# The last expert stage written out over its 32 units, with the next batch routed between them

## The reference, cut to what matters

```
scores = sigmoid(xf @ gate_w.T);  biased = scores + expert_bias
_, sel = top_k(biased, 2);        top_scores = take_along_axis(scores, sel)
routed_in = xf[token_ids] * scores_sorted[:, None]
h = square(relu(grouped_mm(bf16(routed_in), bf16(w_up))))
routed_out = grouped_mm(bf16(h), bf16(w_down))
shared_out = square(relu(xf @ shared_w_up.T)) @ shared_w_down.T
x = layernorm(x + routed_out summed over a token's two experts + shared_out)
```

## Time and profile before

| | us |
|---|---|
| median of 3 runs | 2268.89 (2267.15 to 2275.46) |
| the profiled execution | 2276.37 |
| its span | 2274.5 |
| PE busy in the span | 1954.7 (86%) |
| DVE busy | 1663.7 (73%) |
| ACT busy | 1097.9 (48%) |
| POOL busy | 545.5 (24%) |
| last stage, from its first load to the end of the span | 2098.8 to 2274.5 |

### The profile page before, as it was taken

How to read it: one execution, slowest core, us unless ns; L and a number is a source line. 1 busy time by engine, 2 the same in 40 slices (tenths; PEclk the granted TensorE clock), 3 DMA queues, 4 the chain that set the end, 5 groups by cost and what they waited for, 6 DMA issues and landing times. The chain is left out here.

```text
span 2274.5 us, 31782 instructions
## 1 busy us (share of the span) xinstructions
PE 1954.7 (86%) x10146; PEld 1263.0 (56%) x10146; DVE 1663.7 (73%) x4032; ACT 1097.9 (48%) x2397; POOL 545.5 (24%) x624
## 2 busy tenths in 40 slices
PE   8999799956589999489999999998679988893997
PEld 5666644424367777357666766666453444443544
DVE  4555458866628888668899899888444989996576
ACT  3433345533245555166566666555204756663343
POOL 2222124432201222200000000000001777775111
PEclk9999989976689999689999999999858999996888
DMA  2000000020120000000000000000310222222100
GB/s 84 28 28 18 12 29 21 15 101 28 47 95 10 10 20 10 10 19 1 6 15 6 1 15 6 1 6 6 138 63 9 54 56 70 60 62 73 38 28 28
DMA packets 37238, 75.30 MB, mean 33 GB/s; under 512 B 8822, under 2 KB 20286, under 8 KB 36342
## 3 DMA queue, kind: packets, MB, share of 16 engines
q1 hardware_dynamic: 28918, 56.89, 7.2%
q0 software_dynamic: 8192, 16.79, 2.8%
HBM read 58.98 MB, written 14.68 MB: 32 GB/s over the span
## 5 line engine op out<-in xcount | busy, mean ns | idle before, releaser
L1965 ACT ACTIVATE pk_sums<-pk_sum 128x512 f32<-128x512 f32 x448 | 243.3, 596 | 227.1 <-PE pk_sum L2191 214.6
L2067 DVE SCALAR_TENSOR_TENSOR pk_level<-pk_sums,pk_least 128x1024 f32<-128x1024 f32 x256 | 324.0, 1276 | 22.5 <-ACT pk_sums L1965 21.3
L2198 PE MATMUL pk_weights<-product_keys_early_ident,pk_level 128*128 128x128 f32 x2048 | 267.4, 273 | 35.8 <-DVE pk_level L2067 35.8
L2419 POOL DMA_INDIRECT tk_values<-top_keys_values,tk_index x256 | 243.7, 952 | 202.3 <-DVE tk_index L2584 124.8
L2198 PEld LDWEIGHTS pk_weights<-product_keys_early_ident,pk_level 128*128 128x128 f32 x2048 | 232.0, 141 | 102.0 <-issue 66.5
L2735 PE MATMUL tk_to_act<-tk_keys,tk_xT 128*128 128x512 f32 x512 | 236.7, 610 | 30.1 <-ACT tk_scores L2484 29.4
L2735 PEld LDWEIGHTS tk_to_act<-tk_keys,tk_xT 128*128 128x128 f32 x512 | 95.8, 195 | 153.0 <-issue 93.8
L2190 PE MATMUL pk_sum<-pk_lay_rows,pk_partsT 96*128 96x512 bf16 x448 | 170.2, 380 | 0.2 <-ACT pk_sums L1965 0.2
L2191 PE MATMUL pk_sum<-pk_lay_columns,pk_partsT 96*128 96x512 bf16 x448 | 169.2, 378 | 0.0
L1647 PEld LDWEIGHTS er_outs<-experts_early_w,er_hT 128*128 128x128 f32 x1024 | 134.0, 192 | 59.8 <-issue 56.4
L2582 DVE MAX8 tk_best<-tk_scores 128x8 f32<-128x4096 f32 x32 | 141.3, 4416 | 14.9 <-ACT tk_scores L2484 14.9
(11 more groups left out here) (398 smaller groups left out, 3714.4 us busy)
## 6 DMA issues: line engine op xcount, KB each, us to landing
tk_scores<-top_keys_compress SPq DMA_DIRECT2D x1, 4096.0 KB, 15.1
tk_values<-top_keys_values,tk_index POOLq DMA_INDIRECT x256, 2.5
att_x_proj<-x_first SPq DMA_DIRECT2D x4, 512.0 KB, 5.0
att_x_res<-x_first SPq DMA_DIRECT2D x4, 512.0 KB, 4.1
x_after_attention<-att_y SPq DMA_DIRECT2D x4, 512.0 KB, 4.7
moe_x<-x_after_attention SPq DMA_DIRECT2D x4, 512.0 KB, 3.9
x_after_experts<-moe_y SPq DMA_DIRECT2D x8, 256.0 KB, 2.0
lin_x<-x_after_experts SPq DMA_DIRECT2D x4, 512.0 KB, 4.3
```

The costliest lines, as they stand in the source:

```text
L1965: act.activation(sums[:, n % SUMS, half * HALF:(half + 1) * HALF], bank[:], ACT.Copy).then_inc(S.free.sem, 1)
L2067: dve.scalar_tensor_tensor(level[:, n % LEVELS, :], sums[:, n % SUMS, :], least[:, t % 2, h:h + 1], sums[:, n % SUMS, :], ALU.is_ge, ALU.m ...
L2198: ins = pe.matmul(weights[:, ch * P:(ch + 1) * P], level[:, n % LEVELS, ch * P:(ch + 1) * P], ident[:], is_transpose=True, start=h == 0 an ...
L2419: pool.indirect_dma_start(out=values[:, slot, k, :], out_offset=None, in_=c["values"], in_offset=bass.IndirectOffsetOnAxis(ap=index[slot][ ...
```

## The change

The stage does the same work on the same tiles, in another order and with other banks. The loop over batches is gone: every engine's list is written out over `ALL = 32` units, and the steps of the next batch (transposes and copy of x, gates, exponents, scores, shared up products, relu and squares, transposes of the parts) are placed behind given units of the current one. x has three slots, and the residual reads them, so x is loaded once; `xT` and `partsT` have two slots. The down products and the shared down products keep the expert's matrix as weights and move 512 hidden columns; the sum is then transposed (features on partitions), so ACT copies it (`outT`), PE turns it back by 4 float32 transposes into a bank of its own (`turned`), and DVE adds the residual from there. That bank is taken from ring A, which has 2 banks instead of 3. A batch is stored in halves. In the diff, "..." marks what is left out.

```diff
-        to_act = [m.psum(f"to_act{i}", [P, HALF]) for i in range(3)]
+        to_act = [m.psum(f"to_act{i}", [P, HALF]) for i in range(2)]
...
+        turned = m.psum("turned", [P, HALF])
...
         def _(sp):
-            sp.dma_start(x[:], x_in[0]).then_inc(x_loaded.sem, x_loaded.unit)
...
+            def load(b):
+                after(sp, turned_free, (b - 2) * HALVES)
+                sp.dma_start(x[:, b % 3], x_in[b]).then_inc(x_loaded[b % 3], 16)
+
+            def store(b, g):
+                sp.wait_ge(y_ready, b * HALVES + g + 1)
+                sp.dma_start(x_out[b][:, half_of(g), :], y[:, g]).then_inc(stored[g], 16)
+
+            for b in range(3):
+                load(b)
+            for b in range(B):
+                for g in range(HALVES):
+                    store(b, g)
+                if b + 3 < B:
+                    load(b + 3)
...
         def _(pool):
...
+            for n in range(SHARED):
+                square_shared(0, n)
+            for b in range(B):
+                if b > 0:
+                    root(b - 1, 1)
+                if b + 1 < B:
+                    for n in range(SHARED):
+                        square_shared(b + 1, n)
+                root(b, 0)
+            root(B - 1, 1)
...
         def _(act):
...
+            for unit in range(ALL):
+                b, u = divmod(unit, UNITS)
+                more = b + 1 < B
+                for k in range(PER_UNIT):
+                    take_up(unit, k)
+                if more and u in (0, 1):
+                    take_xT(b + 1, u)
+                if u == 1 and b > 0:
+                    take_out(b - 1, 1)
+                if more and u == 2:
+                    exponents(b + 1)
+                if more and u in (4, 5):
+                    for i in range(2):
+                        take_shared(b + 1, 2 * (u - 4) + i)
+                if u == 5:
+                    take_out(b, 0)
+                if more and u == 5:
+                    take_partsT(b + 1)
+            take_out(B - 1, 1)
...
         def _(dve):
...
+            for unit in range(ALL):
+                b, u = divmod(unit, UNITS)
+                more = b + 1 < B
+                if unit + 1 < ALL:
+                    scale(unit + 1)
+                for k in range(PER_UNIT):
+                    square(unit, k)
+                if u == 2 and b > 0:
+                    finish(b - 1, 1)
+                if u == 3 and b > 0:
+                    normalise(b - 1, 1)
+                if more and u == 3:
+                    score_of(b + 1)
+                if more and u == 4:
+                    parts_of(b + 1)
+                if u == 6:
+                    finish(b, 0)
+                if u == 7:
+                    normalise(b, 0)
...
         def _(pe):
...
+            def shared_project(b, g):
+                after(pe, outT_ready, (b - 1) * HALVES + g + 1)
+                for tail in range(2):
+                    units, w = (TAIL, shared_down_tail) if tail else (P, shared_down)
+                    pe.wait_ge(s_hidden_ready, b * SHARED + g * 2 + tail + 1)
+                    pe.matmul(outs[g][:], w[0:units, :], s_hidden[0:units, g * 2 + tail, :], start=tail == 0, stop=False)
...
+            def project_up(unit):
+                pair = unit % PAIRS
+                for k in range(PER_UNIT):
+                    bank = claim_A()
+                    if k < 2:
+                        pe.wait_ge(W.free.sem, W.free.value(0, 2 * unit + k + 1))
+                        pe.matmul(bank[:], up[:, 2 * pair + k, :], scaled[:, (2 * unit + k) % 4, :],
+                                  start=True, stop=True).then_inc(A.full.sem, 1)
+                    else:
+                        for e in range(2):
+                            ins = pe.matmul(bank[0:2 * TAIL, :], up_tail[:, 2 * pair + e, :],
+                                            scaled[:, (2 * unit + e) % 4, :], start=e == 0, stop=e == 1)
+                        ins.then_inc(A.full.sem, 1)
+
+            def project_down(unit):
...
+                    pe.wait_ge(hidden_ready, n + 1)
+                    ins = pe.matmul(outs[g][:], w, hidden[0:units, n % HIDDEN_SLOTS, :], start=False,
+                                    stop=pair == PAIRS - 1 and k == PER_UNIT - 1)
...
+            def turn_out(b, g):
+                half = b * HALVES + g
+                pe.wait_ge(outT_ready, half + 1)
+                after(pe, turned_free, half)
+                for i in range(PER_HALF):
+                    ins = pe.transpose(turned[:, i * P:(i + 1) * P], outT[:, g, i * P:(i + 1) * P], ident[:])
+                ins.then_inc(turned_full, 1)
+
+            for g in range(HALVES):
+                transpose_x(0, g)
+            gates(0)
+            for n in range(SHARED):
+                shared_hidden(0, n)
+            transpose_parts(0)
+            widen(0)
+            shared_project(0, 0)
+            for unit in range(ALL):
+                b, u = divmod(unit, UNITS)
+                more = b + 1 < B
+                if unit + 1 < ALL:
+                    widen(unit + 1)
+                project_up(unit)
+                if unit >= DOWN_LAG:
+                    project_down(unit - DOWN_LAG)
+                if more and u in (0, 1):
+                    transpose_x(b + 1, u)
+                if u == 2 and b > 0:
+                    turn_out(b - 1, 1)
+                if more and u == 2:
+                    gates(b + 1)
+                if u == 3:
+                    shared_project(b, 1)
+                if more and u in (4, 5):
+                    for i in range(2):
+                        shared_hidden(b + 1, 2 * (u - 4) + i)
+                if more and u == 5:
+                    transpose_parts(b + 1)
+                if u == 6:
+                    turn_out(b, 0)
+                if more and u == 7:
+                    shared_project(b + 1, 0)
+            for unit in range(ALL - DOWN_LAG, ALL):
+                project_down(unit)
+            turn_out(B - 1, 1)
```

More of the change, by code:

```diff
@@ L2757, in routed_experts_stage @@
     UNITS = HALVES * PAIRS
+    ALL = B * UNITS
     DOWN_LAG = 2
@@ new lines, in take_shared, with take_partsT @@
+            def take_shared(b, n):
+                units = P if n % 2 == 0 else TAIL
+                act.wait_ge(A.full.sem, A.to_take(0))
+                bank = A.take()
+                after(act, s_hidden_ready, (b - 1) * SHARED + n + 1 if b else 0)
+                act.activation(s_relu[0:units, n, :], bank[0:units, :], ACT.Relu).then_inc(A.free.sem, 1)
+            def take_partsT(b):
+                act.wait_ge(partsT_full, b + 1)
+                act.activation(partsT[:, b % 2, :], parts_bank, ACT.Copy).then_inc(partsT_ready, 1)
@@ new lines, in take_up, with take_out @@
+            def take_up(unit, k):
+                n = unit * PER_UNIT + k
+                units = 2 * TAIL if k == PER_UNIT - 1 else P
+                act.wait_ge(A.full.sem, A.to_take(0))
+                bank = A.take()
+                after(act, hidden_ready, n - 2 * PER_UNIT + 1)
+                act.activation(relu[0:units, n % (2 * PER_UNIT), :], bank[0:units, :], ACT.Relu).then_inc(A.free.sem, 1)
+            def take_out(b, g):
+                half = b * HALVES + g
+                act.wait_ge(out_full, half + 1)
+                after(act, turned_full, half - 1)
+                act.activation(outT[:, g, :], outs[g][:], ACT.Copy).then_inc(outT_ready, 1)
@@ L2894, in _ @@
                 steps.link(dve.tensor_tensor(score[:], score[:], biased[:], ALU.mult))
-                split_in_three(steps, dve, score[:], lambda i: parts[:, :, i * E:(i + 1) * E], rest[:]).then_inc(parts_ready.sem, parts_ready.unit)
-                def scale(u):
-                    g = u // PAIRS
-                    for k in range(2):
-                        dve.wait_ge(W.full.sem, W.to_take(b))
-                        bank = W.take()
-                        dve.tensor_tensor(scaled[:, (2 * u + k) % 4, :], bank[:], xT[:, g * HALF:(g + 1) * HALF],
-                                                    ALU.mult).then_inc(W.free.sem, 1)
@@ L2942, in _, with scale @@
-                finish(1)
-                normalise(1).then_inc(y_ready.sem, y_ready.unit)
-                steps.restart()
+                after(dve, partsT_ready, b)
+                split_in_three(steps, dve, score[:], lambda i: parts[:, :, i * E:(i + 1) * E], rest[:]).then_inc(parts_ready, 1)
+            def scale(unit):
+                b, u = divmod(unit, UNITS)
+                if unit >= 2:
+                    dve.wait_ge(A.full.sem, made_for_A("up", unit - 2, PER_UNIT - 1))
+                dve.wait_ge(A.free.sem, taken_from_A("xT", b, u // PAIRS))
+                for k in range(2):
+                    dve.wait_ge(W.full.sem, W.to_take(0))
+                    bank = W.take()
+                    dve.tensor_tensor(scaled[:, (2 * unit + k) % 4, :], bank[:], xT[:, b % 2, columns_of(u // PAIRS)],
```

(31 more changed lines are left out.)

288 lines of the change are left out of this document (103 added, 185 removed).

## The result

| kernel | median of its runs, us | ratio of after to before, 95% interval |
|---|---|---|
| before | 2268.0 (2261.8 to 2275.5, 6 runs) | |
| after | 2258.2 (2253.8 to 2259.6, 6 runs) | 0.9951 [0.9929, 0.9973] |

The change made the kernel about 10 us faster; 2270 us was forecast. The profiled execution took 2258.22 us (span 2256.4) against 2276.37 (2274.5). Of the 18 us between the two, 2.46 came about ahead of the last stage, whose first DVE cast is at 2096.37 us instead of 2098.83, and 15.7 in it: 160.0 us from that cast to the end instead of 175.7.

The account below looks back on a forecast made before the run. At full clock PE and DVE were both taken to be at their bound before, PE after. The new order's -14, clock falls' +12 and +3 for POOL and stalls made +1 us, applied to the median: 2270 us, range 2253 to 2287.

Parts of the forecast that it names:

- falls behind the gates: Last stage, next batches' gates: 2.6 falls to half clock, 4.7 us each in the mean, 12 us in all.
- The bank: Ring A with 2 banks: the tail product waits for ScalarE, up to tail 1.12 us for 0.45, +0.67 a unit.
- The down products: Each unit's three products of 512 columns instead of 12 of 128: saving 0.02 us a unit, to 0.75.
- rival 4: Down products: weight loads are what the twelve cost, so -0.58 us a unit, -18, 2252 us; chance 0.04.
- The start: Start of the last stage: widening, two shared down products and widening again put the first up product at 2119.2 us.
- The bound: Last stage: PE carries 35.5 us a batch and bounds it; DVE's 28 a batch fits in that.
- rival 3: Last stage: DVE becomes the bound through POOL's squares, all 12 exposed, 1.02 us each: 2280 us; chance 0.11.
- The list: PE's work from the first up product to the last, units plus next batches' extras, at full clock: 128.4 us.
- POOL beside DVE: POOL's 12 squares beside DVE's work: between 0 and 12 us on DVE, 2 us taken on the path.
- its -14: The new order at full clock, from start to finish of the last stage: 2260.5 us, 14.0 less than 2274.5.
- Rival 1: Last stage: the clock holds or falls once, -14 + 2 us at most, 2256 us; chance 0.25.
- Rival 2: Last stage: after a fall the clock stays low through unit 7, 16 us instead of 4.7, 2281 us; chance 0.17.

Follow-up runs that it names:

- old down products and 3 banks: Changed kernel with 12 down products of 128 columns as before, no turning back, third bank in ring A: 2349.5 us, 0.9871 of the kernel before.
- old down products: Changed kernel with 12 down products of 128 columns as before, no turning back, still 2 banks: 2364.7 us (0.9944), again 2367.2 us (0.9949 of the kernel before).
- gates twice: Changed kernel with the 8 gate products of the next batch run twice in a row: 2378.5 us, 0.9998 of the kernel before.
- filling around the gates: Kernel before with 16 extra bf16 products of 512 columns a batch, before, between and after the gates: 2273.9 us, 1.0029 of the kernel before.
- third run of after: The changed kernel itself, unaltered, measured in a third set on another chip: 2372.0 us, 0.9975 of the kernel before.

## Why the prediction was wrong, point by point

The forecast was +1 us, the medians differ by -10. The step that failed is one term of the sum, the clock's: falls behind the gates were to cost 12 us, 4.7 each, and cost 2.9 in the profile, 1.26 and 1.63. A few small terms leaned the same way.

**Right.** *The bank.* +0.62 a unit came for +0.65 (2.82 and 2.85); up to tail 1.08 for 1.12, since ScalarE starts 0.43 us behind the up product and not 0.51. In the loop with 2 banks and the same down products as before a unit takes 2.93, written out 2.85, so writing out gives 0.08 us a unit back; this the prediction had not seen. *The down products*: 0.74 for 0.75. *The weight loads* (rival 4) cost nothing: 12 products in 0.77 us against 3 in 0.74. The Trainium skill, "TensorE: Matmul & The Clock Gate", Back-to-back issue gap, would by its figures for 128 and 512 columns have had the twelve cost more than twice the three, an estimate, and rival 4's 0.58 us a unit came from there alone; here the measurement decides. *The start*: the record of the first up product is missing, but it follows the widening at 2116.12 by 0.53, at 2116.65; with 2.46 us for the earlier stages 2119.1, predicted 2119.2. *The bound*: PE; rival 3 is out.

**The list.** From the first up product to the last, 2116.65 to 2243.93, it is 127.3 us. Less the 2.9 of the two falls (below) that is 124.4, where 128.4 stood: the pairs of float32 products take 1.91 and 1.86 us in chain for 2.0, the gates 1.7 to 1.85 for 1.95, the unit 0.03 less. In one unit of three batches ScalarE's copy of `partsT` comes between, and the tail waits 0.92 instead of 0.47; that is the stall for which 1 us was added, and it is within the 124.4. The end, from the last up product:

```profile
2243.93 0.59 PE L3097 MATMUL moe_to_act<-moe_scaled,moe_up 128*128 128x512 bf16 x2
...
2248.27 0.66 PE L3121 MATMUL moe_turned<-experts_early_ident,moe_outT 128*128 128x128 f32 x4 [0.69 <-ACT moe_outT L2926]
...
2248.96 0.69 DVE L3001 TENSOR_TENSOR moe_r<-moe_turned,moe_x 128x512 f32<-128x512 f32 x1 [0.17 <-PE moe_turned L3121]
```

is 12.5 us to 2256.4, for 4.8 + 8.0.

**POOL beside DVE**, 2 us for nothing. The contention is there, as the earlier trace rows had it, but on a small instruction; DVE and POOL in order of time:

```profile
2136.10 0.23 DVE L236 TENSOR_TENSOR moe_rest<-moe_score,moe_parts 128x64 f32<-128x64 f32 x1
...
2136.59 1.11 DVE L238 TENSOR_TENSOR moe_parts<-moe_rest,moe_parts 128x64 bf16<-128x64 f32 x1
2136.59 2.03 POOL L2870 TENSOR_TENSOR moe_s_hidden<-moe_s_relu 128x512 f32<-128x512 f32 x2 [23.01 <-ACT moe_s_relu L2908]
2137.63 1.27 DVE L2986 TENSOR_TENSOR moe_scaled<-moe_scores_wide,moe_xT 128x512 bf16<-128x512 f32 x2
```

The line L238 takes 0.23 us alone and 1.0 to 1.1 in the three batches where a square stands beside it: 2.6 us more in all. Otherwise the squares fell beside `scaled`, which takes 0.68 us each with them and without; no `hidden` of this profile stood beside one (0.41 to 0.43 us each, all 93 records). And DVE then waits for PE's `scores_wide` all the same, as the list of waits above shows. With old down products and 3 banks the squares do meet `hidden`, some of which take 1.1 to 1.3 us there.

**The clock, the step that failed.** 2.6 falls at 4.7 us were to cost 12 (the mean of the 2.9 and 5.9 that it gave would have been 4.4, 11 in all). The number of falls was nearly right: in the six profiles of kernels that keep the tail's wait on PE (after three times, old down products twice, gates twice) 13 of 18 gate stretches were followed by a fall, 2.2 a run (one of the 18 stood in the long stretch at half clock already); in the four profiles of the written-out order without that wait it was 2 of 12. The price was not. The first fall's unit, in order of time:

```profile
2124.34 1.85 PE L3055 MATMUL moe_gate_bank<-experts_early_gate,moe_xT 128*128 128x8 f32 x16
2126.12 0.60 PE L3088 MATMUL moe_scores_wide<-moe_partsT,moe_lay 24*128 24x512 bf16 x2
2126.66 0.89 PE L3097 MATMUL moe_to_act<-moe_scaled,moe_up 128*128 128x512 bf16 x2
2127.81 1.09 PE L3101 MATMUL moe_to_act<-moe_scaled,moe_up_tail 128*96 128x512 bf16 x2 [0.26 <-ACT moe_relu L2920]
...
2129.97 1.17 PE L3072 MATMUL moe_outs<-moe_s_hidden,xperts_early_shared_down 128*128 128x512 f32 x2
2131.07 1.12 PE L3072 MATMUL moe_outs<-moe_s_hidden,s_early_shared_down_tail 48*128 48x512 f32 x2
2132.12 0.60 PE L3088 MATMUL moe_scores_wide<-moe_partsT,moe_lay 24*128 24x512 bf16 x2
```

From `scores_wide` to `scores_wide` it is 6.00 us; the same unit of batch 3 at full clock takes 4.74 (2216.73 to 2221.47). So this fall costs 1.26 us. It begins at about 2126.8, behind the gates as predicted, and is over at 2130.2, when the float32 pair that was to lift it has run for 0.2 us, not when the pair or the next one has ended. In 3.4 us at half clock no more than 1.7 can be lost, and part of that is hidden here: the tail's wait is 0.26 us instead of 0.47, as ScalarE is no slower. The second fall, from 2164.4 to 2167.8, begins behind the tail, whose wait is 0.47 as ever, and costs more:

```profile
2162.07 0.60 PE L3088 MATMUL moe_scores_wide<-moe_partsT,moe_lay 24*128 24x512 bf16 x2
...
2165.18 1.91 PE L3072 MATMUL moe_outs<-moe_s_hidden,xperts_early_shared_down 128*128 128x512 f32 x2
...
2168.44 0.60 PE L3088 MATMUL moe_scores_wide<-moe_partsT,moe_lay 24*128 24x512 bf16 x2
```

Its unit takes 6.37 us, 1.63 above 4.74. The two falls cost 2.9 us, 9.1 less than the sum had. Of the 13, eleven lasted 3.0 to 3.5 us, one 7, one 14.

The other side of the account held. Of the 51 us at half clock in the stage before, 38 lay in three stretches of 7, 20.5 and 10 us that followed PE's wait for the first `scaled` of a batch (from 2122.7, 2197.7 and 2242.1), and 13 in two stretches that the prediction put behind the gates. They began among them: 0.9 us after the first gate product of batch 1 (2145.65, fall at 2146.5) and 1.6 us in batch 3 (2226.93, fall at 2228.5), so what PE did ahead of the gates may have had its part in them. The written-out order has one such wait, at the stage's start, instead of four, and the sum had their loss in its -14, since it built the new order at full clock; then it put 12 back. That the order removes them is shown by old down products with 3 banks (no fall) beside the kernel before with the same products and banks (51 us), one profile each; over their runs it is 446 us against 480. That it is PE's idle time at these places which starts them is not shown: the waits for the first `scaled` were never filled, and filling around the gates took 11 us off the half clock.

**The sum again** for the profiled execution, from the forecast's 2276.4 + 1: -9.1 for the clock, -4.0 -0.3 for list and end, -3 for POOL and stalls, -2.5 for earlier stages makes 2258.5; measured 2258.2. It has to come out near, since its terms are read from that profile.

**Applied to the median**, the same corrections, but for the earlier stages', give 2270 - 16.4 = 2253.6, and 2258.2 was measured. The profile of before was not a typical run: 391 us at half clock in all, where 17 later runs have 356 in the mean (344 to 368). Among those runs the time goes with the half clock at 0.32 us per us, so its 35 us are about 11 us, more than the 7.5 that it stands above the median. (On the two other chips the same fit gives 0.18 and 0.46, so this is a rough price.) So of the 18 us between the two profiles some 8 are the one profile's bad luck with the clock, in this stage or ahead of it. The prediction named this and put it, rightly, on the upper side; it was luck for the forecast, which without it would have missed the median by 16 us and not 12.

**The gain in one line.** After has 29 us less half clock than before (327 for 356); at 0.32 us each, or at the 0.46 of a unit (1 - 2.20/4.06), that is 9 to 13 us, an estimate, and 9.8, 7.7 and 7.3 were measured by the medians of the three comparisons. At one clock the two kernels would be level or after a little slower, an estimate too: 160.0 less 2.9 against 175.7 less 22.

**Rivals.** Rival 1, given 0.25, is what came in its effect and not in its mechanism: the falls came and were cheap. Its 2256 is 2 us off. Rival 2's long fall came in one of three profiles of after (20.5 us, which cost some 8 us: 22.5 less 16.0, and 1.3 that the 16.0 hold). How often it comes is not known from three.

## What to carry to other kernels

When a profile shows stretches at half clock, list each with what PE did just before, and price a change by which of these places it removes; a fall that remains is worth at most half its own length. Before a ring gives up a bank, write down the time from its first product to the release of its bank (here 1.1 us) and what PE has to do meanwhile: either leave the third bank, by sharing one that is idle then, or put other products into the wait; each gave 15 to 19 us of the stage back. Take the clock's share of the one profiled execution against that of the other runs before a difference is read off it.

## What was not expected of the hardware

- The clock can stay at half for 14 to 20 us with PE busy nearly without a pause (14.00 of 14.00 us above, 20.40 of 20.40 in the earlier trace rows, 18.9 of 20.5 in the third run of after), and rise elsewhere within 3.4 us.
- ScalarE starts 0.43 us behind the up product where the lists are written out and 0.51 us where they run in the loop; with a bank to wait for this is 0.08 us a unit, 2.85 for 2.93. What in the loop costs it is not shown.
- At half clock the wait for ScalarE shrinks (0.26 for 0.47 us), so that a fall over that wait cost 1.26 us in 3.4, and one that began behind it 1.63.
- The same DVE instruction on 64 columns of two SBUF tiles takes 0.23 us alone and 1.0 to 1.1 beside POOL's square, while `scaled`, which reads one tile from PSUM, takes 0.68 us either way.
- The same kernel takes 2265 us on one chip and 2380 on two others, and the time lies in the one stage that scores the keys.
